# The loops of TensorE's program regrouped: an inner loop over the pair of steps, one choice of projection per group

## The chip, the cores and the metric

One core of a Trainium2 chip runs the whole program. The metric is the device time of one execution in microseconds (us), the median of several runs. PE is TensorE, PEld its weight loads, PEldq the register and branch instructions in the same queue, DVE is VectorE, ACT is ScalarE, POOL is GpSimd, SP is the queue that issues the transfers.

## The reference, cut to what matters

Input x has 2 sequences of 2048 steps with 512 features; `cond` is one vector of 512 per sequence. Four layers follow each other, each with a residual.

```
h0 = cond;  for t: h = tanh(h @ Wh0 + x[t] @ Wx + b)          # a plain recurrence,     x = x + h
w  = softmax over the 2 sequences of (cond . x)/sqrt(512)     # one weight per step,    x = x + x*w
m  = tanh(x @ W_ih.T + cond @ W_hh.T + biases)                # the middle layer,       x = x + m
g0 = cond;  for t: z = sigmoid([x,g] @ Wz + bz);  r = sigmoid([x,g] @ Wr + br)
            c = tanh([x, r*g] @ Wh + bh);  g_new = (1-z)*g + z*c                        # x = x + g_new
            g = tanh(g_new @ Wp + bp) after each 4th step (but the last), else g_new    # "propagation"
```

## The kernel before

The 2048 steps are cut into 128 chunks of 16 steps (`CHUNKS`, `STEPS`). The gated recurrence runs two chunks (`LAG`) behind the plain one, so that in chunk i the program does one step of each, side by side, 16 times. What lies between the two recurrences (softmax over the sequences, middle layer, projection of the gates' inputs) is done for a whole chunk at once, at steps of chunk i that are fixed by hand. Every engine has its own queue in program order, and semaphores that count steps tie the queues together.

**TensorE.** `step` issues four products for one step: `ps_r` (gate r), `ps_z` (gate z), `ps_c` (candidate) and `ps_l` (the plain recurrence, weights and state in three bf16 parts). `ps_r` waits for the state that VectorE's scan leaves (`h_odd` for the first step of a pair, `h_even` for the second). `propagation` is one more product after each 4th step. `softmax_logits` (`ps_proj` from `qx_sum`), `project_mid` (`ps_mid` from `ih`), `project_gates` (`ps_mid` from `rcz_x`, 384 columns) and `project_rnn_input` (`ps_proj` from `rnn_x`) are the chunk's other products.

From chunk 2 on, this is a loop nest with registers: L559 over chunks i, L560 over the four groups q of a chunk, L561 over the two pairs of steps v of a group. The body of the innermost loop is one pair of steps, written out, and behind it a tree of branches (L565 to L581):

```
for v in 0, 1:                       # L561
    two steps
    if v < 1:                        # L565
        if q < 1: softmax_logits     # L566;  else (L568) nothing
    else:
        propagation
        q 0: project_mid;  q 1: project_gates, first half;  q 2: second half;  q 3: project_rnn_input
```

The first two chunks are written out (only the plain recurrence), and the last two (only the gated one) have a nest of the same form at L587. At the head of an iteration the registers for the waits are worked out from i, q and v in one record (FUSED_REGOPS at L561).

**The other engines.** VectorE and ScalarE run a loop over chunks with the 16 steps written out. In a step VectorE transposes each product out of PSUM and ScalarE applies tanh; VectorE's scan (L776) makes the new state. The chunk's extra work stands behind `z_T` of one step: logits and the pair's maximum at u = 2, the reciprocal at u = 3, `mid_T` at u = 5, gate rows at u = 12 and 13. ScalarE does Exp at the end of u = 2 and `mid_tanh` at the start of u = 6. GpSimd adds the results to `y` one step at a time and does the adds and multiplies of softmax and middle layer between them. SP spills and fetches the rows that seed the products.

Of the kernel before, what the change touches and what calls it, by code (L numbers as in the profile page):

```python
# [35 lines left out]
P = 128  # L36
QUAD = 32
NJ = P // QUAD
KT = D // P
STEPS = QUAD // B  # L40
# [12 lines left out]
def cond_resid_kernel(nc, xT, condT, w_rnn_x, w_rnn_h, b_rnn, w_ih, w_hh, b_ih, b_hh,  # L53
# [5 lines left out]
    with ctx:  # L59
# [260 lines left out]
        def _(pool):  # L320
# [29 lines left out]
            def iteration(i):  # L350
# [21 lines left out]
                outputs(i, gru, range(0, 2))  # L372
# [9 lines left out]
                outputs(i, gru, range(2, 3))  # L382
# [8 lines left out]
                outputs(i, gru, range(3, 5))  # L391
# [7 lines left out]
                outputs(i, gru, range(5, 6))  # L399
# [3 lines left out]
                outputs(i, gru, range(6, STEPS))  # L403
# [9 lines left out]
        def _(pe):  # L413
# [95 lines left out]
            def project_gates(i, tiles):  # L509
                if tiles[0] == 0:  # L510
                    pe.wait_ge(x3_new_done, i)
                last = product(ps_mid, ROWS, lambda k: x3_new[:, k, :], lambda k, j: rcz_x[:, k, j, :], 3 * P, tiles)
                if tiles[-1] == KT - 1:
                    last.then_inc(gates_in_product, 1)
# [21 lines left out]
            def projections(i, q):  # L536
                if q == 0:
                    project_mid(i)
                if q in (1, 2):
                    project_gates(i, ((0, 1), (2, 3))[q - 1])  # L540

            for i in range(LAG):
                if i == 1:
                    pe.wait_ge(loaded_gru, 16 * 8)
                for u in range(STEPS):
                    step(True, False, STEPS * i + u, None, u)
                    if i > 0 and u == 1:
                        softmax_logits(i)
                    if u % PROP == PROP - 1:
                        if i > 0:  # L550
                            projections(i, u // PROP)
                        if u // PROP == 3:
                            project_rnn_input(i + 2)
# [5 lines left out]
            with nc.Fori(LAG, CHUNKS, engines=[pe.engine], head_slot={pe.engine: 0}) as i:  # L559
                with nc.Fori(0, GROUPS, engines=[pe.engine]) as q:  # L560
                    with nc.Fori(0, PROP // 2, engines=[pe.engine]) as v:  # L561
                        t = STEPS * i + PROP * q + 2 * v
                        for u in range(2):
                            step(True, True, t + u, t + u - STEPS * LAG, u)
                        with pe.If(v < 1):  # L565
                            with pe.If(q < 1):  # L566
                                softmax_logits(i)
                            with pe.Else():  # L568
                                pe.nop()
                        with pe.Else():  # L570
                            propagation(STEPS * i + PROP * q + PROP - 1 - STEPS * LAG)
                            with pe.If(q < 2):
                                with pe.If(q < 1):
                                    projections(i, 0)
                                with pe.Else():
                                    projections(i, 1)
                            with pe.Else():
                                with pe.If(q < 3):
                                    projections(i, 2)
                                with pe.Else():  # L580
                                    with pe.If(i < CHUNKS - 2):  # L581
                                        project_rnn_input(i + 2)
                                    with pe.Else():
                                        pe.nop()


            with nc.Fori(CHUNKS, CHUNKS + LAG, engines=[pe.engine], head_slot={pe.engine: 0}) as i:  # L587
                with nc.Fori(0, GROUPS, engines=[pe.engine]) as q:
                    with nc.Fori(0, PROP // 2, engines=[pe.engine]) as v:
                        t = STEPS * i + PROP * q + 2 * v  # L590
                        for u in range(2):
                            step(False, True, None, t + u - STEPS * LAG, u)
                        with pe.If(v < 1):
                            with pe.If(STEPS * i + q < STEPS * CHUNKS + 1):
# [340 lines left out]
```

## Time and profile before

| | |
|---|---|
| median of 3 runs | 8982.6 us (8972.62 to 8989.48) |
| the profiled execution | 8973.57 us, its span 8971.7 us |
| PE busy | 8283.6 us, 92% of the span |
| PEld busy | 7582.6 us, 85% |
| DVE busy | 5908.8 us, 66% |
| ACT busy | 4568.0 us, 51% |
| POOL busy | 1071.9 us, 12% |
| mean granted clock of TensorE | 0.995 |

Busy time of PE is that of matmuls that overlap (each takes 0.22 us or more and the next starts long before it ends), so gaps between products are read from start times rather than from busy shares.

### The profile page before, as it was taken

Reading aid. Unit: us, or ns where it says so; the run is one execution under the profiler, and the core shown is the slowest. Engines: PE = TensorE matmul, PEld = TensorE weight load, DVE = VectorE, ACT = ScalarE, POOL = GpSimd, SP = SyncE. Lnnn points to the kernel's source line nnn. Section 1 sums busy time; section 2 is a strip of 40 time slices with the busy share of each in tenths; the row PEclk is TensorE's granted clock in tenths of the full one; section 3 lists DMA queues with packets and bytes.
Section 4 is the critical chain, followed back from the end, with each engine's and each line's share of the span. In section 5 each row is a group of like instructions: output and inputs, shape, how many; then the busy total and the mean of one; then the engine's idle time right before and its main releaser. Section 6 shows DMA issues by size and latency. Waiting matters only on the chain.

```text
span 8971.7 us, 1050872 instructions
## 1 busy us (share of the span) xinstructions
PE 8283.6 (92%) x472080; PEld 7582.6 (85%) x472080; DVE 5908.8 (66%) x34722; ACT 4568.0 (51%) x26367; POOL 1071.9 (12%) x4362
## 2 busy tenths in 40 slices
PE   6999999999999999999999999999999999999998
PEld 5888888888888888888888888888888888888887
DVE  4666666666666666666666666666666666666665
ACT  3555555555555555555555555555555555555554
POOL 1111111111111111111111111111111111111110
PEclk8999999999999999999999999999999999999999
DMA  1000000000000000000000000000000000000000
GB/s 64 10 11 11 10 10 11 12 10 10 11 12 10 10 11 12 10 10 11 12 10 10 11 12 10 10 10 12 10 10 10 13 10 10 10 13 10 10 10 8
DMA packets 133303, 104.84 MB, mean 12 GB/s; under 512 B 14976, under 2 KB 132096, under 8 KB 132096
## 3 DMA queue, kind: packets, MB, share of 16 engines
q1 hardware_dynamic: 133248, 104.20, 3.8%
q8 instruction: 23, 0.38, 0.0%
q14 instruction: 32, 0.26, 0.0%
HBM read 62.20 MB, written 41.94 MB: 12 GB/s over the span
## 4 chain that ended last, share of the span: by engine, by line
PE 92%; issue 7%; DVE 1%; ACT 0%; DMA 0%; SPq 0%; DVEq 0%; ACTq 0%; POOL 0%
PE ps_c L453 27%; PE ps_r L453 23%; PE ps_z L430 20%; PE ps_l L441 16%; PE ps_mid L419 6%; PE ps_proj L419 2%; DVE ps_c L628 0%; PE ps_proj L502 0%; DVE l_T L624 0%; DMA rnn_h<-w_rnn_h 0%; ACT scan_add L866 0%; ACT rnn_hist L828 0%; DVE l_pre L677 0%; DVE l_parts L695 0%; DVE rnn_h L662 0%
## 5 line engine op out<-in xcount | busy, mean ns | idle before, releaser
L453 PE MATMUL ps_c<-c_h,rh 128*2 128x64 f32 x131072 | 2209.7, 219 | 0.3 <-issue 0.3
L453 PEld LDWEIGHTS ps_c<-c_h,rh 128*2 128x2 f32 x131072 | 2037.8, 85 | 14.3 <-issue 0.5
L849 ACT ACTIVATE r_tanh<-ps_r 128x4 f32<-128x4 f32 x4096 | 711.7, 174 | 2500.0 <-DVE ps_r L628 2423.2
L628 DVE STREAM_TRANSPOSE ps_r<-ps_r 128x64 f32<-128x64 f32 x4096 | 1087.2, 265 | 1341.9 <-PE ps_r L453 1217.4
L441 PE MATMUL ps_l<-rnn_h_parts,l_parts 128*6 128x128 bf16 x98304 | 1763.8, 220 | 48.8 <-DVE l_parts L695 42.6
L628 DVE STREAM_TRANSPOSE ps_c<-ps_c 128x64 f32<-128x64 f32 x5118 | 1352.4, 264 | 680.3 <-PE ps_c L453 651.5
L453 PEld LDWEIGHTS ps_r<-r_h,h_odd 128*2 128x2 f32 x65536 | 918.0, 85 | 830.6 <-issue 469.6
L453 PE MATMUL ps_r<-r_h,h_odd 128*2 128x64 f32 x65536 | 1103.5, 219 | 547.4 <-issue 539.2
L441 PEld LDWEIGHTS ps_l<-rnn_h_parts,l_parts 128*6 128x6 bf16 x98304 | 1488.3, 86 | 57.3 <-ACT ps_l L788 48.5
L453 PE MATMUL ps_r<-r_h,h_even 128*2 128x64 f32 x65536 | 1109.3, 219 | 14.7 <-DVE h_even L776 8.8
L430 PE MATMUL ps_z<-z_h,h_odd 128*2 128x128 f32 x32768 | 1088.5, 273 | 0.0
L430 PE MATMUL ps_z<-z_h,h_even 128*2 128x128 f32 x32768 | 1082.3, 273 | 0.0
L453 PEld LDWEIGHTS ps_r<-r_h,h_even 128*2 128x2 f32 x65536 | 906.6, 84 | 94.6 <-DVE h_even L776 39.1
L866 ACT ACTIVATE scan_add<-ps_c 128x4 f32<-128x4 f32 x4096 | 717.8, 175 | 447.0 <-DVE ps_c L628 277.6
L729 DVE SCALAR_TENSOR_TENSOR rh<-r_tanh,h_neg_half 128x4 f32<-128x4 f32 x4096 | 678.9, 166 | 352.1 <-ACT r_tanh L849 351.9
L430 PEld LDWEIGHTS ps_z<-z_h,h_odd 128*2 128x2 f32 x32768 | 825.4, 85 | 15.7
L430 PEld LDWEIGHTS ps_z<-z_h,h_even 128*2 128x2 f32 x32768 | 810.2, 85 | 25.3
L860 ACT ACTIVATE z_tanh<-z_T 128x8 f32<-128x8 f32 x2048 | 429.4, 210 | 599.3 <-DVE z_T L624 599.3
L624 DVE STREAM_TRANSPOSE z_T<-ps_z 128x128 f32<-128x128 f32 x2048 | 647.6, 316 | 59.5 <-PE ps_z L430 10.4
L624 DVE STREAM_TRANSPOSE l_T<-ps_l 128x128 f32<-128x128 f32 x2048 | 632.4, 309 | 46.7 <-PE ps_l L441 46.7
L343 POOL TENSOR_TENSOR y<-x,h_even 128x8 f32<-128x8 f32 x1024 | 212.7, 208 | 3712.9 <-DVE h_even L776 3696.1
L453 PE MATMUL ps_c<-prop_w,h_pre 128*2 128x64 f32 x32704 | 593.9, 219 | 3.7 <-DVE h_pre L776 3.7
(87 smaller groups left out, 9165.5 us busy)
## 6 DMA issues: line engine op xcount, KB each, us to landing
gates_spill<-gates_rows SPq DMA_DIRECT2D x128, 192.0 KB, 1.9
gates_seeds<-gates_spill SPq DMA_DIRECT2D x512, 48.0 KB
x_next<-xT SPq DMA_DIRECT2D x128, 64.0 KB, 1.7
x_mid<-xT SPq DMA_DIRECT2D x128, 64.0 KB, 1.7
rnn_spill<-rnn_rows SPq DMA_DIRECT2D x128, 64.0 KB, 1.5
rnn_seeds<-rnn_spill SPq DMA_DIRECT2D x512, 16.0 KB
y_out<-y SPq DMA_DIRECT2D x128, 64.0 KB, 1.6
rcz_x<-w_rc_x SPq DMA_DIRECT2D x1, 2048.0 KB, 9.2
```

The source lines that it names most:

```text
L343: tt(y[:, :, rows], x3[:, :, rows], h[:, :, :, 1], ALU.add).then_inc(y_ready, 1)
L419: last = nc.tensor.matmul(psum[QUAD * j:QUAD * j + rows, 0:width], stationary(k), weights(k, j), start=(k == 0), stop=(k == KT - 1))
L430: last = nc.tensor.matmul(psum[QUAD * j:QUAD * j + B, 0:P], stationary(k), w[:, k, P * j:P * (j + 1)], start=False, stop=(k == KT - 1), sk ...
L441: last = nc.tensor.matmul(psum[QUAD * j:QUAD * j + PARTS * B, 0:P], state_parts[:, k, :, :].rearrange("p q b -> p (q b)"), w_parts[:, k, j ...
L453: last = nc.tensor.matmul(pair[QUAD * j:QUAD * j + B, n, at:at + W], stationary(k), w[:, k, P * j + W * n:P * j + W * (n + 1)], start=Fals ...
L624: return nc.vector.transpose(tile, psum[:, 0:P])
L628: nc.vector.transpose(pieces[n].rearrange("p k r -> p (k r)"), pair[:, n, at:at + W]).then_inc(T_done[n], inc)
L729: nc.vector.scalar_tensor_tensor(rh[:, k, :], r_tanh[:, k, :], 1.0, h_neg_half[:, k, :], ALU.subtract, ALU.mult).then_inc(rh_ready[n], 1)
L849: nc.scalar.activation(r_tanh[:, k, :], r_T[n][:, :, 0:B], ACT.Tanh, scale=-0.5).then_inc(r_tanh_done[n], 1)
L860: nc.scalar.activation(z_tanh[:, :, :], z_T[:, :, 0:B], ACT.Tanh, scale=0.5).then_inc(z_tanh_done, 1)
L866: nc.scalar.activation(scan_add[:, k, :, 0], c_T[n][:, :, 0:B], ACT.Tanh).then_inc(c_tanh_done[n], 1)
```

## The change

The loop over q now holds three parts one behind the other: a loop over the two pairs of steps with nothing but the pair in it (its counter is the step number itself, with an offset), then the propagation, then one tree of branches that picks the chunk's other product: `softmax_logits` for q 0, `project_mid` for q 1, all of `project_gates` for q 2, `project_rnn_input` for q 3. Softmax so moves from behind step 1 to behind step 3, the middle layer from behind step 3 to behind step 7, and the gates' projection, halved until now behind steps 7 and 11, stands whole behind step 11. The last two chunks and the written-out chunk 1 follow the same order. VectorE, ScalarE and GpSimd take up their parts later: logits at u = 4, Exp at u = 4, reciprocal at u = 5, `mid_T` at u = 8, `mid_tanh` at u = 9; GpSimd's steps are moved in the same way between its sums. No product, transfer or vector operation is added or removed.

```
@@ GpSimd: the same work between the outputs
-                outputs(i, gru, range(0, 2))
+                outputs(i, gru, range(0, 4))
...
-                outputs(i, gru, range(2, 3))
+                outputs(i, gru, range(4, 5))
...
-                outputs(i, gru, range(3, 5))
+                outputs(i, gru, range(5, 8))
...
-                outputs(i, gru, range(5, 6))
+                outputs(i, gru, range(8, 9))
...
-                outputs(i, gru, range(6, STEPS))
+                outputs(i, gru, range(9, STEPS))
@@ TensorE: the projection of the gates in one piece
-            def project_gates(i, tiles):
-                if tiles[0] == 0:
-                    pe.wait_ge(x3_new_done, i)
-                last = product(ps_mid, ROWS, lambda k: x3_new[:, k, :], lambda k, j: rcz_x[:, k, j, :], 3 * P, tiles)
-                if tiles[-1] == KT - 1:
-                    last.then_inc(gates_in_product, 1)
+            def project_gates(i):
+                pe.wait_ge(x3_new_done, i)
+                product(ps_mid, ROWS, lambda k: x3_new[:, k, :], lambda k, j: rcz_x[:, k, j, :], 3 * P).then_inc(gates_in_product, 1)
@@ TensorE: the main nest
             with nc.Fori(LAG, CHUNKS, engines=[pe.engine], head_slot={pe.engine: 0}) as i:
                 with nc.Fori(0, GROUPS, engines=[pe.engine]) as q:
-                    with nc.Fori(0, PROP // 2, engines=[pe.engine]) as v:
-                        t = STEPS * i + PROP * q + 2 * v
+                    behind = STEPS * i + (PROP * q + 2 - STEPS * LAG)
+                    with nc.Fori(behind, behind + PROP, 2, engines=[pe.engine]) as t:
                         for u in range(2):
-                            step(True, True, t + u, t + u - STEPS * LAG, u)
-                        with pe.If(v < 1):
-                            with pe.If(q < 1):
-                                softmax_logits(i)
-                            with pe.Else():
-                                pe.nop()
-                        with pe.Else():
-                            propagation(STEPS * i + PROP * q + PROP - 1 - STEPS * LAG)
-                            with pe.If(q < 2):
-                                with pe.If(q < 1):
-                                    projections(i, 0)
-                                with pe.Else():
-                                    projections(i, 1)
-                            with pe.Else():
-                                with pe.If(q < 3):
-                                    projections(i, 2)
-                                with pe.Else():
-                                    with pe.If(i < CHUNKS - 2):
-                                        project_rnn_input(i + 2)
+                            step(True, True, t + (u - 2 + STEPS * LAG), t + (u - 2), u)
+                    propagation(behind + (PROP - 3))
+                    with pe.If(q < 2):
+                        with pe.If(q < 1):
+                            softmax_logits(i)
+                        with pe.Else():
+                            project_mid(i)
+                    with pe.Else():
+                        with pe.If(q < 3):
+                            project_gates(i)
+                        with pe.Else():
+                            with pe.If(i < CHUNKS - 2):
+                                project_rnn_input(i + 2)
...
@@ VectorE, in the written-out steps
-                    if mid and u == 5:
+                    if mid and u == 8:
                         dve.wait_ge(mid_product, i)
                         transposed(flat(mid_T[:, :, :]), ps_mid).then_inc(mid_T_done, 1)
...
-                    if mid and u == 2:
+                    if mid and u == 4:
                         dve.wait_ge(logit_product, i)
...
-                    if mid and u == 3:
+                    if mid and u == 5:
                         dve.wait_ge(denom_done, i)
@@ ScalarE
-                    if mid and u == 6:
+                    if mid and u == 9:
                         act.wait_ge(mid_pre_done, i)
...
-                    if mid and u == 2:
+                    if mid and u == 4:
                         act.wait_ge(shifted_done, i)
```

## Rows read from the trace of the kernel before

**Rows 1.** Windows: one chunk; busy per engine, granted clock.

```profile
core 0: us, PE busy (x) PEld busy (x) DVE busy (x) ACT busy (x) POOL busy (x), PEclk, DMA share, GB/s
4000.00:4069.00 69.00, 64.42 (x3699) 59.06 (x3693) 46.01 (x272) 35.70 (x208) 8.32 (x34) 1.00 0.03 10
```

**Rows 2.** Waits of PE, 200 to 8820 us (total, times, longest), then from 8820.

```profile
PE ps_r L453 <- issue: 519.4, 748, 1.8
...
PE ps_r L453 <- issue: 10.9, 7, 2.1
```

**Rows 3.** Timeline of PE: l to the next product, within and between pairs.

```profile
4014.61 0.85 PE L441 MATMUL ps_l<-rnn_h_parts,l_parts 128*6 128x128 bf16 x48
4015.31 1.09 PE L453 MATMUL ps_r<-r_h,h_even 128*2 128x64 f32 x64
...
4017.98 0.85 PE L441 MATMUL ps_l<-rnn_h_parts,l_parts 128*6 128x128 bf16 x48
4019.61 1.07 PE L453 MATMUL ps_r<-r_h,h_odd 128*2 128x64 f32 x64 [0.77 <-issue]
...
4069.98 0.85 PE L441 MATMUL ps_l<-rnn_h_parts,l_parts 128*6 128x128 bf16 x48
4070.65 0.27 PE L502 MATMUL ps_proj<-qx_sum,ones 128*32 128x32 f32 x8
4071.48 1.07 PE L453 MATMUL ps_r<-r_h,h_odd 128*2 128x64 f32 x64 [0.56 <-issue]
```

**Rows 4.** Source lines in PE's queue, 4018.3 to 4019.7 us; durations in ns.

```profile
L565 PEldq COMPARE_BRANCH  x1: 67/67/67, 4018.4 to 4018.4; - x1
L566 PEldq COMPARE_BRANCH  x1: 207/207/207, 4018.5 to 4018.5; - x1
L568 PEldq COMPARE_BRANCH  x1: 169/169/169, 4018.8 to 4018.8; - x1
L561 PEldq ALU_OP  x1: 36/36/36, 4019.0 to 4019.0; - x1
L561 PEldq COMPARE_BRANCH  x1: 209/209/209, 4019.1 to 4019.1; - x1
L561 PEldq FUSED_REGOPS  x1: 160/160/160, 4019.4 to 4019.4; - x1
```

**Rows 5.** The same for L560, 4011 to 4012 us.

```profile
L560 PEldq MOVE  x1: 35/35/35, 4011.6 to 4011.6; - x1
```

**Rows 6.** Timeline of PE: ends of the groups q 0, q 1 and q 3.

```profile
4008.56 0.85 PE L441 MATMUL ps_l<-rnn_h_parts,l_parts 128*6 128x128 bf16 x48
4009.35 1.23 PE L453 MATMUL ps_c<-prop_w,h_pre 128*2 128x64 f32 x64
4010.43 1.08 PE L419 MATMUL ps_mid<-ih,x 128*32 128x128 f32 x32
4011.95 1.07 PE L453 MATMUL ps_r<-r_h,h_odd 128*2 128x64 f32 x64 [0.43 <-issue]
...
4025.64 0.85 PE L441 MATMUL ps_l<-rnn_h_parts,l_parts 128*6 128x128 bf16 x48
4026.43 1.15 PE L453 MATMUL ps_c<-prop_w,h_pre 128*2 128x64 f32 x64
4027.56 1.50 PE L419 MATMUL ps_mid<-rcz_x,x_new 128*32 128x384 f32 x16
4028.89 1.07 PE L453 MATMUL ps_r<-r_h,h_odd 128*2 128x64 f32 x64
...
4059.55 0.85 PE L441 MATMUL ps_l<-rnn_h_parts,l_parts 128*6 128x128 bf16 x48
...
4063.78 1.07 PE L453 MATMUL ps_r<-r_h,h_odd 128*2 128x64 f32 x64 [0.80 <-issue]
```

**Rows 7.** Timeline of DVE and ACT, 4018.3 to 4019.7 and 4026.3 to 4029.0 us.

```profile
4018.50 0.48 DVE L776 TENSOR_TENSOR_SCAN h_odd<-scan_mul,scan_add 128x8 f32<-128x8 f32 x2
...
4019.00 0.30 ACT L845 ACTIVATE mid_tanh<-mid_pre 128x128 f32<-128x128 f32 x1
...
4028.07 0.17 ACT L879 ACTIVATE h_odd<-ps_c 128x4 f32<-128x4 f32 x1 [0.25 <-DVE ps_c L628]
```

**Rows 8.** Source line L566 over the whole span; min/median/max in ns.

```profile
L566 PEldq COMPARE_BRANCH  x630: 65/202/3604, 127.9 to 8818.7; - x158
```

More of the change, by code:

```diff
@@ L546, in _ @@
                     step(True, False, STEPS * i + u, None, u)
-                    if i > 0 and u == 1:
+                    if i > 0 and u == 3:
                         softmax_logits(i)
[L549 to L552, printed above, removed]
-                            project_rnn_input(i + 2)
+                    if i > 0 and u == 7:
+                        project_mid(i)
+                    if i > 0 and u == 11:
+                        project_gates(i)
+                    if u == 15:
+                        project_rnn_input(i + 2)
             pe.wait_ge(r_seeded, 1)
@@ L587, in _ @@
             with nc.Fori(CHUNKS, CHUNKS + LAG, engines=[pe.engine], head_slot={pe.engine: 0}) as i:
                 with nc.Fori(0, GROUPS, engines=[pe.engine]) as q:
-                    with nc.Fori(0, PROP // 2, engines=[pe.engine]) as v:
-                        t = STEPS * i + PROP * q + 2 * v
+                    behind = STEPS * i + (PROP * q + 2 - STEPS * LAG)
+                    with nc.Fori(behind, behind + PROP, 2, engines=[pe.engine]) as t:
                         for u in range(2):
-                            step(False, True, None, t + u - STEPS * LAG, u)
-                        with pe.If(v < 1):
-                            with pe.If(STEPS * i + q < STEPS * CHUNKS + 1):
-                                softmax_logits(CHUNKS)
-                            with pe.Else():
-                                pe.nop()
-                        with pe.Else():
-                            with pe.If(STEPS * i + PROP * q < STEPS * (CHUNKS + LAG) - PROP):
-                                propagation(STEPS * i + PROP * q + PROP - 1 - STEPS * LAG)
-                            with pe.Else():
-                                pe.nop()
-                            with pe.If(STEPS * i + q < STEPS * CHUNKS + 2):
-                                with pe.If(STEPS * i + q < STEPS * CHUNKS + 1):
-                                    projections(CHUNKS, 0)
-                                with pe.Else():
-                                    projections(CHUNKS, 1)
-                            with pe.Else():
-                                with pe.If(STEPS * i + q < STEPS * CHUNKS + 3):
-                                    projections(CHUNKS, 2)
-                                with pe.Else():
-                                    pe.nop()
@@ new lines, in _ @@
+                            step(False, True, None, t + (u - 2), u)
+                    with pe.If(STEPS * i + PROP * q < STEPS * (CHUNKS + LAG) - PROP):
+                        propagation(behind + (PROP - 3))
+                    with pe.Else():
+                        pe.nop()
+                    with pe.If(STEPS * i + q < STEPS * CHUNKS + 2):
+                        with pe.If(STEPS * i + q < STEPS * CHUNKS + 1):
+                            softmax_logits(CHUNKS)
+                        with pe.Else():
+                            project_mid(CHUNKS)
@@ L614, in _ @@
+                    with pe.Else():
+                        with pe.If(STEPS * i + q < STEPS * CHUNKS + 3):
+                            project_gates(CHUNKS)
+                        with pe.Else():
+                            pe.nop()
         @block.vector
```

9 lines of the change are left out of this document (3 added, 6 removed).

## The prediction

> **What bounds the kernel now.** I looked first at the busy time of one chunk, then at PE's waits, then at the order of its products in time, last at the register and branch records of its queue. In a chunk of 69.00 us PE is busy 64.42 us at the full granted clock, DVE 46.01 and ACT 35.70 [rows 1]: PE sets the pace. Between 200 and 8820 us it waits almost only for "issue" in front of `ps_r`: 519.4 us in 748 places [rows 2]. The reader is to see where: inside a pair the next `ps_r` starts 0.70 us after `ps_l` (4014.61 to 4015.31); between the pairs of a group it takes 1.63 us (4017.98 to 4019.61), and 1.50 us where softmax's product stands between them (4069.98 to 4071.48) [rows 3]. No data is late there: the scan that makes `h_odd` is done at 4018.98 [rows 7], 0.6 us before `ps_r` starts. The queue is busy with control: six records from 4018.4 to the load at 4019.60 [rows 4]. Their durations sum to 0.85 us, the distance is 1.2 us, so each brings about 0.06 us more to the next. Prices per record, from [rows 4, 5]: compare that falls through 0.067 + 0.06 = 0.13; compare that jumps (L566, and L561's back edge) 0.27; plain jump (L568) 0.23; ALU_OP 0.10; MOVE 0.09; FUSED_REGOPS 0.22. The first of them comes 0.42 us after `ps_l` starts (4017.98 to 4018.4): the queue runs some 0.2 us ahead of the array, and control longer than that shows.
>
> **The inner edge, four per chunk.** Before, one takes 1.50 and three take 1.63 us from `ps_l` to `ps_r` [rows 3]; sum 6.39. The change removes the compare L565 (0.13), the compare L566 (0.27), the jump L568 (0.23) and the index arithmetic of the head (0.22), since the counter is the step number and `ps_r`'s wait needs it unchanged. What is left is one addition (0.10) and the back edge (0.27); the head must still copy the counter (a MOVE, 0.09). So 0.42 + 0.10 + 0.27 + 0.09 = 0.88. The loop's limit is now a register, for which there is no row: nothing if it is kept, one ALU_OP (0.10) if it is worked out at each edge. I take 0.90. Four edges: 3.60. Gain 6.39 - 3.60 = 2.79 us per chunk. Floor: the 0.70 of a pair's inside, where data sets the start; ceiling 0.98.
>
> The Trainium skill (Advanced Engine Details and Errata, Control Flow Timing) gives about 51 ns for a branch and 108 ns for a compare-and-branch. By it the three removed branches would be 0.27 us instead of 0.63, four edges would give 1.4 us less, and the time would be about 8820. The rows show 169 ns and 207 ns for those that jump, and 67 ns for one that doesn't; the measurement decides.
>
> **The ends of the groups.** Before, from `ps_l` to the next `ps_r`: 3.39 (q 0), 3.25 (q 1; q 2 has the same pattern and is taken as 3.25), 4.23 (q 3) [rows 6]; sum 14.12. Afterwards:
> - The way to the propagation stays 0.79 (4008.56 to 4009.35): a jumping compare and an addition become an addition, a compare that falls through and an addition, 0.04 less, which the wait for `h_pre` takes up. From the propagation to the next product it is 1.13 with a jumping compare (4026.43 to 4027.56), so 0.99 with two that fall through.
> - Behind the chosen product there stood: jump, addition, compare falling through, addition, back edge, two MOVEs, index arithmetic = 0.23 + 0.10 + 0.13 + 0.10 + 0.27 + 0.18 + 0.22 = 1.23. Now: jump, addition, back edge, index arithmetic, one MOVE = 0.91. That is 0.32 less. I assume that copying q, start value and limit fit into the one fused record; if each operation is a record of its own, some seven at 0.10 cost 0.5 more.
> - q 0 (softmax): 0.79 + 0.99 + what follows softmax today, 4070.65 to 4071.48 = 0.83 [rows 3], plus the MOVE = 2.70. `h_odd` comes from the propagation here, and softmax is short cover. In q 1 its second half is written from 4028.07 to 4028.24 [rows 7], 1.81 us behind the propagation's start at 4026.43; `ps_r` would start after 0.99 + 0.92 = 1.91, so the state is there by 0.1 us.
> - q 1 (middle layer): 0.79 + 1.13 + (4010.43 to 4011.95 = 1.52, less 0.32) = 3.12.
> - q 2 (all gates): 16 matmuls of 384 columns occupy 1.33 us (4027.56 to 4028.89), and cover their control; 32 take at most 2.66, of which the start-up is paid once: 2.60. 0.79 + 1.13 + 2.60 = 4.52.
> - q 3: 4.23 - 0.32 = 3.91.
>
> Sum 14.25, that is 0.13 more than before: the ends come out even, since one control sequence covered by gates' matmuls is traded for softmax's uncovered one. Net 2.79 - 0.13 = 2.66 us per chunk.
>
> **The moved steps.** VectorE's logits stay behind the first step of a pair (u 2 to 4), and their cost there is the same. The reciprocal goes from u = 3 to 5, ahead of an edge, which is no worse. `mid_T` goes from u = 5 (ahead of an edge with slack) to u = 8 (ahead of a step within a pair); I charge 0.03 us per chunk, at the most the 0.3 that a transpose lasts. `mid_tanh` on ScalarE ran at 4019.00 for 0.30 us [rows 7], 0.5 us after the scan began. At u = 9 the next `ps_r` starts sooner, but ScalarE is wanted only when that product has been transposed, some 1.1 us later, so it stays hidden. GpSimd's part is nearly idle (8.32 of 69 us, [rows 1]) and is asked for one group later, by queues that have a group's time. SP issues the same transfers.
>
> **The sum.** 126 chunks x (2.66 - 0.03) = 331 us. The last two chunks have no `ps_l`, so `ps_r` waits for data longer; all their issue waits are 10.9 us [rows 2], of which I take half, 5. The first chunks: nothing. 331 + 5 = 336. Against the profiled execution's own time: 8973.6 - 336 = 8637.6. The median of the runs stands 9 us above that execution: 8646 by it. I forecast 8640.
>
> **The rivals.**
> - More is won: the edge meets the 0.70 to 0.75 of the inside of a pair, if copy and limit cost nothing or PE's queue gets further ahead. For: nothing else stood in the way inside a pair. Against: the records have to run. 4 x 0.17 x 126 = 86 us more, 8555. Chance 0.10.
> - Less is won, by register work: limit at each edge and the heads' arithmetic unfused: (0.08 x 4 + 3 x 0.48) x 126 = 222 us less, 8860. For: a register limit and a computed start are new. Against: seven operations fit in one record now. Chance 0.10.
> - Less is won, because VectorE and ScalarE needed the pauses. They have 46 us of work in a chunk that would last 66.4, but each step's chain is serial. Against: second steps of a pair run with no pause before them, on time. If half of each edge's gain were eaten: 2.79 / 2 x 126 = 176 us less, 8815. Chance 0.06.
> - Slower: the back jumps miss the code. The longest compare at L566 took 3.604 us, its median 0.202 [rows 8]: a first arrival at cold code. If each group's back jump (four per chunk) paid 3.4 us, the chunk would be 13.6 - 2.6 = 11 us longer, about 10,000 in all. It decides from 0.66 us per group on. Against: today's innermost back edge spans more code than the new one, at 209 ns. Chance 0.04.
> - The change does not do this, since something else holds the edge at today's length: 8970 to 8985. Chance 0.02.
>
> The Trainium skill (Runtime: NRT & Kernel Launch, Instruction fetch mechanics) says that a jump to code outside the current two pages stalls on a fetch, which is the fourth rival's mechanism. The trace shows such a stall only in L566's maximum.
>
> **How the numbers follow.** The forecast as worked out has 0.68; its own range is 8590 to 8700 (edge 0.85 to 0.98, heads 0.1 either way, `mid_T` up to 0.3). To leave out no more than 2 in 10, I take 8555 to 8745: with it go the first rival and the milder cases of the second. A difference of 0.2% (18 us) is about what a measurement of this kernel can tell from none. Faster 0.93, the same 0.03, slower 0.04.
>
> **What would show it.** Right: between the pairs `ps_l` to `ps_r` of about 0.90 us in place of 1.63, behind softmax about 0.9 us, `ps_proj<-qx_sum` now behind the propagation; two records and a MOVE at each edge, and a chunk of 66.4 us. Wrong: waits for DVE in front of `ps_r`, compare records of microseconds in every chunk, or edges that stay above 1.1 us.

## The result, and the profile after

| | before | after |
|---|---|---|
| median of the runs | 8986.04 us (4 runs, 8972.62 to 8992.95) | 8619.63 us (4 runs, 8616.62 to 8622.46) |
| profiled execution | 8973.57, span 8971.7 | 8622.46, span 8620.6 |
| mean granted clock | 0.995 | 0.995 |

The ratio is 0.9594, with an interval of 0.9577 to 0.9611: faster by 4.1%, 20 us below the 8640 forecast and inside the range.

First the page of after: span and instructions, busy times, and the queue that fetches code.

```profile
span 8620.6 us, 1049320 instructions
PE 8290.4 (96%) x472080; PEld 7617.0 (88%) x472080; DVE 5914.3 (69%) x34722; ACT 4570.1 (53%) x26367; POOL 1073.8 (12%) x4362
q8 instruction: 23, 0.38, 0.0%
```

PE's busy time is what it was (8283.6 and 8290.4 us); only its share rose, from 92% to 96%. The same window of one chunk, which answers to [rows 1] with 66.4 us in place of 69:

```profile
4000.00:4066.40 66.40, 64.50 (x3704) 59.33 (x3693) 46.00 (x272) 35.66 (x207) 8.34 (x34) 1.00 0.04 11
```

What PE waited for between 200 and 8480 us (total, times, longest), against [rows 2]:

```profile
PE ps_r L453 <- ACT h_odd L861: 81.0, 125, 0.6
PE ps_r L453 <- issue: 66.7, 157, 1.5
```

The 519.4 us of "issue" (PE waits for its own queue) in 748 places in front of `ps_r` are 66.7 in 157. What is new there, ScalarE's `h_odd`, is one place per chunk, the end of group q 0; whether that name is right is asked below.

PE's products in time. First an edge between two pairs and the inside of a pair ([rows 3]), then the ends of the groups q 1, q 2, q 3 and q 0 (against [rows 6]); start and duration in us:

```profile
4013.26 0.85 PE L441 MATMUL ps_l<-rnn_h_parts,l_parts 128*6 128x128 bf16 x48
4014.15 1.07 PE L453 MATMUL ps_r<-r_h,h_odd 128*2 128x64 f32 x64
...
4016.80 0.85 PE L441 MATMUL ps_l<-rnn_h_parts,l_parts 128*6 128x128 bf16 x48
4017.51 1.09 PE L453 MATMUL ps_r<-r_h,h_even 128*2 128x64 f32 x64
...
4004.00 0.85 PE L441 MATMUL ps_l<-rnn_h_parts,l_parts 128*6 128x128 bf16 x48
4004.78 1.18 PE L453 MATMUL ps_c<-prop_w,h_pre 128*2 128x64 f32 x64
4005.97 1.08 PE L419 MATMUL ps_mid<-ih,x 128*32 128x128 f32 x32
4007.20 1.07 PE L453 MATMUL ps_r<-r_h,h_odd 128*2 128x64 f32 x64 [0.15 <-issue]
...
4020.18 0.85 PE L441 MATMUL ps_l<-rnn_h_parts,l_parts 128*6 128x128 bf16 x48
4020.97 1.12 PE L453 MATMUL ps_c<-prop_w,h_pre 128*2 128x64 f32 x64
4022.09 2.79 PE L419 MATMUL ps_mid<-rcz_x,x_new 128*32 128x384 f32 x32
4024.68 1.09 PE L453 MATMUL ps_r<-r_h,h_odd 128*2 128x64 f32 x64
...
4037.70 0.85 PE L441 MATMUL ps_l<-rnn_h_parts,l_parts 128*6 128x128 bf16 x48
4038.45 1.15 PE L453 MATMUL ps_c<-prop_w,h_pre 128*2 128x64 f32 x64
4040.06 1.08 PE L419 MATMUL ps_proj<-rnn_x,x_next 128*32 128x128 f32 x32 [0.45 <-issue]
4041.63 1.07 PE L453 MATMUL ps_r<-r_h,h_odd 128*2 128x64 f32 x64 [0.48 <-issue]
...
4054.75 0.85 PE L441 MATMUL ps_l<-rnn_h_parts,l_parts 128*6 128x128 bf16 x48
4055.50 1.16 PE L453 MATMUL ps_c<-prop_w,h_pre 128*2 128x64 f32 x64
4056.52 0.27 PE L502 MATMUL ps_proj<-qx_sum,ones 128*32 128x32 f32 x8
4057.44 1.07 PE L453 MATMUL ps_r<-r_h,h_odd 128*2 128x64 f32 x64 [0.65 <-ACT h_odd L861]
```

The reader is to see that the edge is 0.89 us (4013.26 to 4014.15) where it was 1.63, with no wait marked on it any more, and that the inside of a pair is the same 0.71. The ends are 3.20 (q 1), 4.50 (q 2), 3.93 (q 3) and 2.69 (q 0).

The control records of that edge, by source line (durations in ns), against [rows 4]; the inner loop is L555:

```profile
L555 PEldq FUSED_REGOPS  x1: 37/37/37, 4013.7 to 4013.7; - x1
L555 PEldq COMPARE_BRANCH  x1: 213/213/213, 4013.8 to 4013.8; - x1
L555 PEldq MOVE  x1: 37/37/37, 4014.1 to 4014.1; - x1
```

Three records where there were six: a fused record that must hold the addition to the counter and the limit (no other record is left for them; the profile does not show what a fused record holds), the back edge, the copy. And at the head of the group behind q 3's projection:

```profile
L552 PEldq MOVE  x1: 35/35/35, 4041.2 to 4041.2; - x1
L552 PEldq FUSED_REGOPS  x1: 152/152/152, 4041.3 to 4041.3; - x1
```

Where the state stands beside them: the first half of VectorE's scan for the edge at 4014.15 and for the inside of the pair at 4017.51, and the second half of ScalarE's `h_odd` for the end of q 0 at 4057.44:

```profile
4013.74 0.17 DVE L758 TENSOR_TENSOR_SCAN h_odd<-scan_mul,scan_add 128x8 f32<-128x8 f32 x1
...
4017.28 0.17 DVE L758 TENSOR_TENSOR_SCAN h_even<-scan_mul,scan_add 128x8 f32<-128x8 f32 x1
...
4057.16 0.17 ACT L861 ACTIVATE h_odd<-ps_c 128x4 f32<-128x4 f32 x1 [0.25 <-DVE ps_c L610]
```

Inside a pair `ps_r` starts 0.06 us behind the end of that scan (0.054 to 0.055 at each of 960 such places in 120 chunks): there data sets the start. At the edge it starts 0.24 us behind it here (median 0.229 of 480): the data is there, and the control is what is late.

**Where the 351 us came from.** The two spans differ by 8971.7 - 8620.6 = 351.1 us. By the starts of the first `ps_r` of the chunks: the first chunk in which both recurrences run starts at 116.92 before and at 120.04 after (-3.1); from there to chunk 126 it is 8574.63 and 8233.69, for 124 chunks 69.15 and 66.40 us each (340.9); the next two chunks, without a projection of the plain recurrence's input, take 138.26 and 133.51 (4.75); the last two, in which only the gated recurrence runs, 137.8 and 129.2 up to the start of the last product (8.5). 340.9 + 4.75 + 8.5 - 3.1 = 351.1.

Within a chunk, medians of the distances from product to product over 123 chunks, and for the chunk their sum:

| us per chunk | before | after | gain | forecast |
|---|---|---|---|---|
| four edges, `ps_l` to `ps_r` | 1.500, 1.623, 1.624, 1.622 = 6.37 | 0.884, 0.884, 0.882, 0.882 = 3.53 | 2.84 | 2.79 |
| ends of q 0, q 1, q 2, q 3 | 3.388, 3.250, 3.240, 4.318 = 14.20 | 2.690, 3.104, 4.502, 3.927 = 14.22 | -0.03 | -0.13 |
| inside the pairs | | | -0.05 | -0.03 |
| chunk | 69.05 | 66.29 | 2.76 | 2.63 |

### The profile page after: what moved, and what is told of

It reads as the page before. It is cut to its first block, busy times and chain, and to the rows that moved or that the text cites. A ratio compares the mean times of both kernels' runs of the same rounds, so it can differ in the third digit from the quotient of the medians.

```text
span 8620.6 us, 1049320 instructions
## 1 busy us (share of the span) xinstructions
PE 8290.4 (96%) x472080; PEld 7617.0 (88%) x472080; DVE 5914.3 (69%) x34722; ACT 4570.1 (53%) x26367; POOL 1073.8 (12%) x4362
## 4 chain that ended last, share of the span: by engine, by line
PE 95%; issue 3%; DVE 1%; ACT 0%; DMA 0%; ACTq 0%; DVEq 0%; SPq 0%; POOL 0%
PE ps_c L453 27%; PE ps_r L453 24%; PE ps_z L430 21%; PE ps_l L441 16%; PE ps_mid L419 6%; PE ps_proj L419 2%; DVE ps_c L610 1%; ACT h_odd L861 0%; DVE l_T L606 0%; DMA rnn_h<-w_rnn_h 0%; ACT scan_add L848 0%; ACT rnn_hist L810 0%; DVE l_pre L659 0%; DVE l_parts L677 0%; ACTq L860 0%
## 5 line engine op out<-in xcount | busy, mean ns | idle before, releaser
L453 PEld LDWEIGHTS ps_r<-r_h,h_odd 128*2 128x2 f32 x65536 | 935.5, 85 | 407.7 <-issue 199.4
L773 ACT ACTIVATE ps_c<-gates_seeds 128x128 f32<-128x128 f32 x2048 | 563.7, 275 | 0.1
```

The lines of the kernel that those rows point to most:

```text
L453: last = nc.tensor.matmul(pair[QUAD * j:QUAD * j + B, n, at:at + W], stationary(k), w[:, k, P * j + W * n:P * j + W * (n + 1)], start=Fals ...
L773: return nc.scalar.activation(pair[:, :, at:at + W], rows.rearrange("p (h n) -> p h n", h=2), ACT.Copy)
```

## The experiments

The theory: PE's queue issues control and matmuls in one order and runs some 0.2 us ahead of the array behind short products; what is gained is the records taken out at the inner edges, and the moves of the projections gain nothing. The rivals: the new placement of the projections is what pays; the state (VectorE's and ScalarE's chain) is what sets the edge now; code fetches count. The kernel before, run beside them, had a median of 8981 to 8985 us. Ratios are to it. Below, "edge" is `ps_l` to the next `ps_r` between pairs, and u is the step within a chunk, 0 to 15.

### The moves without the loops

Before's loops and tree of branches, with after's placement of every step:

```
                    with nc.Fori(0, PROP // 2, engines=[pe.engine]) as v:
                        t = STEPS * i + PROP * q + 2 * v
                        ...
                        with pe.If(v < 1):
                            with pe.If(q < 1):
-                                softmax_logits(i)
+                                pe.nop()
...
                        with pe.Else():
                            propagation(...)
+                           q 0: softmax_logits;  q 1: project_mid;  q 2: project_gates;  q 3: project_rnn_input
```

> The nest of before (innermost loop over the two pairs, tree of branches in its body) with the schedule of after: softmax, middle layer, whole gates and input projection behind the propagations of q 0 to q 3, and the other engines' steps as late as in after. Theory (the gain lies in the control records at the inner edge): edges stay at 1.63 us (1.50 in q 0), 6.39 in all; the ends of the groups are those of after plus 0.32 each where control isn't covered, about 2.7 + 0.3, 3.2 + 0.3, 4.5, 3.93 + 0.3 = 15.2 against 14.1 before. So 1.1 us per chunk and some 140 us slower than before: 9120. Rival (the later places or the joined gates' projection are what gains): faster than before, below 8950.

Measured: 9120.48 us (9119.05 to 9127.52), ratio 1.0156 [1.0139, 1.0173]. An edge of its timeline:

```profile
4013.79 0.85 PE L441 MATMUL ps_l<-rnn_h_parts,l_parts 128*6 128x128 bf16 x48
4015.41 1.07 PE L453 MATMUL ps_r<-r_h,h_odd 128*2 128x64 f32 x64 [0.77 <-issue]
```

The edges stay at 1.48 (q 0) and 1.62, the chunk is 70.15 us. So the moves by themselves lose 1.1 us per chunk, nearly all of it at the ends of the groups (15.29 us in place of 14.20): three ends now have control that no long product covers, where before two had, and only q 2's end has the gates' product in front of its control. All of the gain, and the repair of this loss, is the shorter control.

### One record more at each edge

```
                        for u in range(2):
                            step(True, True, ...)
+                        with pe.If(i < 3):
+                            pe.nop()
+                        with pe.Else():
+                            pe.nop()
```

> After, with one more compare in the inner loop behind the pair that jumps in every chunk but one, and does nothing. Theory (a record in the queue costs its price fully once the queue's lead is used up): 0.27 us at each of 4 edges and about 0.25 in front of each of 4 propagations, 2.1 us per chunk, 262 us: about 8880. Rival (the edge is set by data or the queue has lead left): less than 0.1 us at each edge, below 8720.

Measured: 8859.42 us (8841.92 to 8863.33), ratio 0.9857 [0.984, 0.9873].

```profile
4006.28 0.85 PE L441 MATMUL ps_l<-rnn_h_parts,l_parts 128*6 128x128 bf16 x48
4007.43 1.08 PE L453 MATMUL ps_r<-r_h,h_odd 128*2 128x64 f32 x64 [0.29 <-issue]
```

The edge goes from 0.884 to 1.146: one jumping compare costs 0.26, as the price list of the prediction has it (0.27). The scan for the next pair now ends 0.49 us before `ps_r` starts, where it was 0.23: the state waits for the control. The four in front of the propagations cost 0.24 to 0.32 there too, of which 0.04 to 0.09 comes back, because the propagation's own second half then finds its data. The chunk is 1.96 us longer. This confirms prices and places; had the state set the edge, the record would have been free.

### The four steps of a group written out

No inner loop at all, so the edge has no control:

```
-                    with nc.Fori(behind, behind + PROP, 2, engines=[pe.engine]) as t:
-                        for u in range(2):
-                            step(True, True, t + (u - 2 + STEPS * LAG), t + (u - 2), u)
+                    for u in range(PROP):
+                        step(True, True, behind + (u - 2 + STEPS * LAG), behind + (u - 2), u % 2)
```

> After, with the four steps of a group written out in the main nest, so that no inner edge is left; the body of the loop over q grows from some 1200 to some 2030 records of PE's queue. Theory: each of the four edges falls from 0.88 us to the 0.71 to 0.75 that a product takes inside a pair, 4 x 0.17 x 126 = 86 us: about 8534. Rival 1 (VectorE and ScalarE need the pauses): some edge stays above 0.8 and a wait for DVE or ACT appears in front of ps_r. Rival 2 (the code must be at hand): issue waits of 1 to 4 us in every group, and a time above 9000.

Measured: 15978.4 us, ratio 1.7788 [1.7758, 1.7818]. The theory's 8534 missed by a factor of nearly two, and the rival of the code fetches won far beyond its bound. Its page (queue, packets, MB, share), then what PE waited for between 200 and 15800 us, then PE's timeline at the end of a group and in the middle of a product:

```profile
q8 instruction: 4553, 74.60, 2.2%
```

```profile
PE ps_r L453 <- issue: 2918.6, 1393, 5.7
PE ps_c L453 <- issue: 1511.9, 1063, 1.9
PE ps_z L430 <- issue: 702.3, 500, 1.6
PE ps_l L441 <- issue: 589.8, 500, 1.5
```

```profile
8009.09 0.27 PE L502 MATMUL ps_proj<-qx_sum,ones 128*32 128x32 f32 x8
8014.48 1.89 PE L453 MATMUL ps_r<-r_h,h_odd 128*2 128x64 f32 x64 [5.12 <-issue]
...
8024.71 0.67 PE L441 MATMUL ps_l<-rnn_h_parts,l_parts 128*6 128x128 bf16 x35 [1.13 <-issue]
```

The queue of code carried 23 packets in after and 4553 here: 4530 more in 504 groups, nine per group, each 74.60 MB / 4553 = 16.4 KB. Five stalls per group, with medians of 1.1 to 1.6 us, stand in the middle of products, and they are 127 or 128 matmuls apart: with their weight loads and the control between them that is 256 records, and each packet carries as many at 64 bytes a record. So a stall stands where a block of 256 records begins. A longer one, 5.1 us here and up to 5.7, stands at the jump back to the group's head. (15978 - 8620) / 504 = 14.6 us per group. A part of it is the clock: its mean is 0.893, against 0.995, and behind the long stall it is granted at 0.50, the lower of its two levels, from 8014.5 to 8019.5 us; there `ps_r` lasts 1.89 us in place of 1.07. How much of the 14.6 us is the clock was not separated. The nest has some 2030 records in PE's queue, after's has 1213 (by a count of the programs; matmuls and weight loads alone are 2000 and 1168), of which nothing is fetched again: between 200 and 8600 us that queue carries 4 packets in after. Where between the two the cliff lies was not tried.

The Trainium skill (Runtime: NRT & Kernel Launch, Instruction fetch mechanics) says that PE holds 2048 instructions, refilled in blocks of 256, and that a jump outside the current two blocks waits for a fetch. The block agrees with the 16.4 KB seen here. By the two blocks after's nest, five of them long, would have to fetch at each back jump; the runs show that it does not. The 2048 alone do not give the cliff either: a nest of some 2030 is below them and is fetched again all the same.

### VectorE's work moved ahead of the edges

Twice, to ask whether VectorE's extra work inside the pairs costs anything, and whether it does ahead of an edge:

```
-                    if u == 0 and mid and next_rnn(i):      # the plain recurrence's rows
+                    if u == 1 and mid and next_rnn(i):
...
-                    if mid and u == 8:                      # mid_T;  mid_tanh 9 -> 10
+                    if mid and u == 9:
...
-                    if mid and u == 4:                      # logits and Exp, first kernel only
+                    if mid and u == 5:
...
-                    if mid and u == 5:                      # reciprocal, first kernel only
+                    if mid and u == 6:
```

> After, with VectorE's extra work moved one step later, so that it stands ahead of an inner edge and not inside a pair: the input rows from u 0 to 1, logits u 4 to 5 (Exp with them), reciprocal 5 to 6, mid_T 8 to 9 (mid_tanh to 10), GpSimd's outputs shifted by one. Theory: inside the pairs it delays ps_r by 0.18, 0.04 and 0.04 us (ps_l to h_even 0.89, 0.75, 0.75 in place of 0.71), and an edge of 0.88 covers that: 0.26 us per chunk, 33 us: about 8587. Rival (the edge has no room either): no difference, 8615 to 8625, with waits for DVE at the edges.

Measured: 8626.99 us (8626.08 to 8630.75), ratio 0.9605 [0.9589, 0.9621]: a miss by 40. The rows' move gives its 0.08 (behind `ps_l` at u = 0: 0.887 to 0.807) and `mid_T`'s its 0.03 (0.044, of which 0.013 comes back in the next product), but the reciprocal now stands inside a pair, and `ps_r` to `ps_z` at u = 7 grew from 0.905 to 1.016; the logits' move gives 0.01 only, since what `ps_r` starts earlier it then waits for the second half of the state. The ends of q 1 and q 3 take 0.015 and 0.045 more, which the edit does not explain.

The second kernel moves only rows and `mid_T`:

> The run before of this kind, with two of its three moves only: the input rows from u 0 to 1 and mid_T from 8 to 9 (mid_tanh to 10); logits, Exp and reciprocal stay as in after, since the reciprocal at u = 6 stood inside a pair and cost 0.11 us there. Theory: 0.08 and 0.03 us per chunk, 14 us: 8606. Rival (what is won inside the pair is lost at the edge): 8615 to 8625.

Measured: 8604.04 us (8603.24 to 8607.52), ratio 0.9578 [0.9562, 0.9594]. That is 16 us less than after; forecast as 14. Rows give 0.08 and `mid_T` 0.04 per chunk. 8 ns at each edge (0.876) came with them; they are not the moves' doing, since the next kernel, which moves nothing on VectorE, has the same 0.876. So a part of the 16 us may not be the moves' either.

### Half of the middle layer's product

```
-                product(ps_mid, ROWS, lambda k: x2[:, k, :], columns(ih)).then_inc(mid_product, 1)
+                product(ps_mid, ROWS, lambda k: x2[:, k, :], columns(ih), P, (0, KT - 1)).then_inc(mid_product, 1)
```

> After, but the middle layer's product leaves out two of its four input tiles (16 of 32 matmuls), so the output isn't the reference's. The product stands in q 1 in front of 0.91 us of control. Theory (it mostly covers control): 0.54 us of matmuls fall away, but the next ps_r can start only 0.91 us behind the jump, so ps_mid to ps_r falls from 1.16 to about 1.0 us: 0.15 to 0.2 us per chunk, 20 to 25 us: 8597. Rival (matmul time is what counts): 0.54 x 126 = 68 us: 8552.

Measured: 8621.1 us, ratio 0.9596 [0.9577, 0.9615], where 8597 was expected. PE's timeline at the ends of q 1 and q 2:

```profile
4005.96 0.64 PE L419 MATMUL ps_mid<-ih,x 128*32 128x128 f32 x16
4006.96 1.07 PE L453 MATMUL ps_r<-r_h,h_odd 128*2 128x64 f32 x64 [0.35 <-issue]
...
4020.69 1.15 PE L453 MATMUL ps_c<-prop_w,h_pre 128*2 128x64 f32 x64
4022.06 2.79 PE L419 MATMUL ps_mid<-rcz_x,x_new 128*32 128x384 f32 x32 [0.21 <-issue]
```

This kernel leaves out two of the middle layer's four input tiles. At q 1 all is as expected: 16 matmuls fewer, some 0.44 us of work, and `ps_mid` to `ps_r` is only 0.18 shorter (1.163 to 0.985): behind it the control sets the time and the product is what is hidden. But at q 2 the propagation to `ps_mid` grew from 1.153 to 1.367, in a place that the edit does not touch. Two later kernels ask why.

### Half of the gates' product

```
-                product(ps_mid, ROWS, ..., lambda k, j: rcz_x[:, k, j, :], 3 * P).then_inc(gates_in_product, 1)
+                product(ps_mid, ROWS, ..., lambda k, j: rcz_x[:, k, j, :], 3 * P, (0, KT - 1)).then_inc(gates_in_product, 1)
```

> After, but the gates' projection leaves out two of its four input tiles (16 of 32 matmuls of 384 columns), so the output isn't the reference's. Theory: half of it still covers its 0.91 us of control, as before the change (1.33 us from ps_mid to ps_r), so all of the matmul time comes back: 2.60 to 1.33, 1.27 x 126 = 160 us: 8460. Rival (control shows again): less than 120 us, above 8500.

Measured: 8453.79 us, ratio 0.941 [0.9391, 0.9429].

```profile
4006.97 1.50 PE L419 MATMUL ps_mid<-rcz_x,x_new 128*32 128x384 f32 x16
4008.27 1.09 PE L453 MATMUL ps_r<-r_h,h_odd 128*2 128x64 f32 x64
```

From 2.596 to 1.306 us: here the full work of 16 matmuls goes (two of the four input tiles are left out of the gates' projection). Behind 384 columns the group's control costs nothing, behind 128 columns of the middle layer it costs what the product does not cover. Both halves of the prediction's reading of the ends so hold.

### The counter used without its copy

The first wait of a pair reads the loop's register itself, and the copy stands behind the first product:

```
+                    with contextmanager(pair_loop)(behind, behind + PROP, 2) as (counter, copied):
+                        halved_product(ps_r, ..., h_odd_ready, counter, r_product, 1)
+                        t = copied()
                        for u in range(2):
-                            step(True, True, ..., u)
+                            step(True, True, ..., u, gate_r=u > 0)
```

> After, with ps_r's first wait in a pair taken straight from the loop's counter register, and the copy of the counter made behind that product, where the queue is ahead. Nothing else changes; one MOVE record is gone from the head. Theory (each record costs its price, here 0.09 us): 0.88 to 0.79 at four edges, and 0.09 at the ends of q 0, q 1 and q 3; q 2 is covered by its matmuls: 7 x 0.09 x 126 = 80 us: 8540. Rival (the edge is at its floor, set by the scan or the start of ps_r): no more than 20 us, above 8600.

Measured: 8565.54 us (8561.8 to 8565.71), ratio 0.9533 [0.9517, 0.9549]. The four edges are 0.790 in place of 0.884: the MOVE, 0.09, was the last thing in front of `ps_r`. So the edges of after are still set by control and not by the state. But the chunk is 0.40 us shorter where 0.63 was taken out of it. The rest is given back, most of it as waits for data: `ps_r` to `ps_z` at u = 6 is 0.930 instead of 0.890 (the second half of the state ends 0.31 to 0.32 us behind the start of `ps_r`, in after 0.22, and the gap stands at the first matmul that needs it), and `ps_l` to `ps_r` at u = 14 is 0.805 instead of 0.709 (`ps_r` starts 0.055 behind the scan); the ends of q 1 and q 3 gain only 0.04 and 0.05. At q 0's end `ps_r` starts 0.085 us earlier than in after, so that the wait which the profile put down to ScalarE's `h_odd` ended with the MOVE: in after its second half is written 0.11 us before `ps_r` starts.

### Counters kept in registers, and that with the vector work moved

Pair counter, limit and the propagation's count live in registers over the whole nest, are raised inside the propagation's product, and the heads have no index arithmetic left; the first wait of a pair reads the counter directly, as in the kernel before this one:

```
+            def bookkeeping():
+                captured[0] = nc.snap(group, ...);  captured[1] = nc.snap(chunk, ...)
+                nc.regs_alu(limit, limit, PROP, op=add)
+                nc.regs_alu(pre, pre, PROP, op=add)
...
+                    halved_product(ps_c, P_AT, ..., prop_w, h_pre_ready, pre, p_product, PROP,
+                                   early=((0, 0), (1, 0)), between=bookkeeping)
```

> After, with the control of the main nest cut down: pair counter, its limit and the propagation's count are registers that run through the whole nest, raised inside the propagation's product where the queue is ahead; so the head of a group works out nothing, and the first waits read the registers directly. Theory: edges 0.88 to 0.79 (0.36 per chunk), behind the chosen product 0.91 to 0.60 us of control (q 1 0.30; q 3 0.39, since the head of a chunk has one record left; q 0 only 0.24, because the propagation's state is then late; q 2 nothing, it is covered), 0.1 in front of the propagations: 1.4 us per chunk, 175 us: 8445. Rival (data sets the starts once control is this short): a wait for ACT or DVE in front of ps_r at every edge, and above 8530.

Measured: 8478.57 us (8476.04 to 8479.21, 5 runs), ratio 0.944 [0.9427, 0.9453].

```profile
4010.53 0.85 PE L441 MATMUL ps_l<-rnn_h_parts,l_parts 128*6 128x128 bf16 x48
4011.32 1.08 PE L453 MATMUL ps_r<-r_h,h_odd 128*2 128x64 f32 x64
```

From the chosen product to `ps_r` it is now 0.613 (q 0), 0.898 (q 1) and 1.212 (q 3), in place of 0.918, 1.163 and 1.566: what was taken out of the heads, the MOVE of 0.09 among it, was worth 0.27 to 0.35 a piece where no long product covers it. The time is 34 us above the expected 8445: the propagations start 0.03 to 0.06 earlier (0.753 to 0.707 behind `ps_l`) and take as much longer or a little more (0.05 to 0.07), and the two late places of the kernel before this one are here too (0.932 at u = 6, 0.808 at u = 14).

With the second kernel's moves of VectorE's work on top:

> The same with VectorE's input rows at u = 1 and mid_T at u = 9. Theory: another 0.11 us per chunk, 14 us: 8431. Rival (an edge of 0.79 us has no room for them any more): the same time as without.

Measured: 8461.43 us (8458.29 to 8463.65, 5 runs), ratio 0.9422 [0.941, 0.9435]. The two gains add up (17 us for the moves, 16 in the kernel without the registers). It leaves out nothing of the reference and is the fastest kernel of the study that leaves out nothing, 5.8% below before and 158 us below after.

### Where the gates' product begins in the code

The nest's first record can be shifted against the blocks of 256 records that the fetching kernel had shown. In the kernel with half of the middle layer's product the gates' matmuls begin 1023 records behind the nest's head, the last record of a block; in after 1055 (both by a count of the program, of which 1008 and 1040 are matmuls and weight loads).

```
-            with nc.Fori(LAG, CHUNKS, engines=[pe.engine], head_slot={pe.engine: 0}) as i:
+            with nc.Fori(LAG, CHUNKS, engines=[pe.engine], head_slot={pe.engine: 96}) as i:     # half of the middle product
...
+            with nc.Fori(LAG, CHUNKS, engines=[pe.engine], head_slot={pe.engine: 224}) as i:    # after itself
```

> The kernel with half of the middle product (which leaves out two of its four input tiles, so the output isn't the reference's) came out at 8621 us, since the gates' first matmul in q 2 started 0.21 us later than in after. Its code had moved: by counting the records of the nest, the gates' block begins 1023 records behind the nest's head (four times 256, less one), and in after 1055. Here the same kernel with the nest's head 96 records further on (head_slot 96 in place of 0). Theory (a product that begins where a fetched stretch of code ends pays about 0.2 us): the 0.21 us is gone, 0.21 x 126 = 27 us: 8595. Rival (it comes from the shorter product itself): 8615 to 8625 as before.

Measured: 8599.44 us (8594.88 to 8604.31), ratio 0.9571 [0.9555, 0.9587]. The first kernel's 0.2 us is gone:

```profile
4006.90 1.16 PE L453 MATMUL ps_c<-prop_w,h_pre 128*2 128x64 f32 x64
4008.06 2.79 PE L419 MATMUL ps_mid<-rcz_x,x_new 128*32 128x384 f32 x32
```

> After, with nothing changed but the nest's head at slot 224, so that the gates' block begins one record short of five times 256. Theory: the gates' first matmul starts 0.2 us later in each chunk, and the time rises by some 27 us: 8647, if the other boundaries stay hidden inside the pair. Rival: 8615 to 8625, the place of the code does not matter.

Measured: 8662.26 us (8657.54 to 8662.71), ratio 0.9638 [0.9622, 0.9654].

```profile
4038.17 1.15 PE L453 MATMUL ps_c<-prop_w,h_pre 128*2 128x64 f32 x64
4039.51 2.79 PE L419 MATMUL ps_mid<-rcz_x,x_new 128*32 128x384 f32 x32 [0.19 <-issue]
```

Put there on purpose, the boundary costs the same 0.20 us per chunk, 25 of the 43 us by which this kernel is slower than after and 15 us more than expected. The code queue carries 23 packets here, as in after: nothing is fetched again. Most of the rest lies behind `ps_l` at u = 2, 8 and 14, 0.04 to 0.05 each, and behind `ps_r` at u = 14, 0.04 (a gap behind its 14th matmul, not at its wait for the second half of the state); that these are boundaries too was not tested. In after the boundaries inside the pairs cost nothing that can be seen. A reading that fits is that a boundary shows where it falls into a stretch of control, since the queue's lead is already used up there; it was not tested by itself, and only this one place, one record short of a multiple of 256, was tried.

## Why the prediction was right

**What bounds the kernel.** Right: PE's queue, by its control records at the edges. One compare more costs what the list says, one MOVE fewer gives what the list says, and the moves without the loops leave the edges where they were. The state was there 0.23 us before `ps_r` started at an edge of after.

**The inner edge.** 0.884 measured, 0.90 forecast from a price list. The step that was open, the price of a limit in a register, came out as nothing: beside the back edge and the copy there is one fused record of 37 ns. Gain 2.84 instead of 2.79.

**The ends.** q 0 2.690 (2.70), q 1 3.104 (3.12), q 2 4.502 (4.52), q 3 3.927 (3.91). The assumption behind them, that the head's seven operations fit in one record, is seen at L552 (one fused record of 152 ns). Within the ends one small step was wrong: the 0.04 less in front of the propagation was to be taken up by the wait for `h_pre`; in q 2 `ps_l` to the propagation fell from 0.785 to 0.753, and it was the propagation itself that took 0.04 more (1.109 to 1.153). The margin of 0.1 us for the state at q 0's end was 0.11. Their sum before was 14.20 and not 14.12: q 3's end took 4.23 in the one chunk that was read, its median is 4.32. So the difference is -0.03 instead of -0.13. At 0.10 x 126 = 13 us this is the largest error of the sum, most of it from reading one sample.

**The moved steps.** 0.05 instead of 0.03 us per chunk, `mid_T` at u = 8 (0.708 to 0.751) being most of it. `mid_tanh` stayed hidden.

**Both ends of the program.** The last two chunks gave 8.5 us instead of 5, the first ones cost 3.1 instead of nothing, which nearly cancels. What in the first chunks takes the 3.1 was not looked for.

**The sum.** The 126 chunks gave 345.7 us where 331 was forecast, 14.7 more, and the two ends of the program 0.4 more; that is the 15.1 us between 8637.6, forecast for the profiled execution, and its 8622.5. The mechanism and the terms were right, and not only the total: none was off by more than 0.10 us per chunk. Edges and ends both came out better than forecast, which is most of the 15. The other 5 us to the 8640 are that this was rounded up from 8637.6 and that the median lies 2.8 us below the profiled execution. Of the last two chunks the 5 us were half of a row, a guess; that they fall short by 3.5 and the first chunks cost 3.1 where nothing was set is a near balance by luck.

**The rivals.** That more is won was false for after: the edge met not the inside of a pair but the MOVE. The kernels without that MOVE and without the heads' arithmetic show how much of it was there to win. Register work: false, one fused record per head. VectorE needing its pauses: false at 0.884, but not empty. At 0.79 the second half of the state begins to be late, by 0.04 to 0.1 at a few places of a chunk, and with what the ends do not give that is a third of the 0.63 us per chunk that was forecast for the MOVE. Back jumps that miss the code: false for after, 23 packets in the whole execution, but a real mechanism one step further: a body of four steps instead of two pays for it in every group. The price set for it, 3.4 us per group, was too low by four times, and its sum was off too: 11 us in each of 126 chunks on 8974 is some 10,360, not 10,000. Such a stall stands in before's trace at two more compares (1.96 us at L559, 1.72 at L594), not only at L566; all three are first arrivals.

## What to carry to other kernels

Where an engine's queue carries control between short products, list the control records with their durations and their distance, and price an edit record by record; read each distance as a median over many repetitions, since one sample was the largest error here. Look at what kind of product stands in front of a control sequence: behind 16 or 32 matmuls of 384 columns it was free here, behind 32 of 128 columns it was not, and leaving out half of that product gave back only 0.18 of its 0.44 us. Before a loop body is written out, count the records of its whole nest.

## What the runs showed of the hardware that was not expected

- A nest of some 2030 records in PE's queue fetches its code again in each iteration (nine packets of 16.4 KB, 14.6 us with the slower clock), one of 1213 fetches none. The stalls stand 127 or 128 matmuls apart, a block of 256 records.
- The stalls of such fetches take the clock along: granted clock 0.893 on average in that kernel, 0.995 in after, and 1.89 instead of 1.07 us for the same 64 matmuls behind a stall of 5.1 us.
- With no code fetched again, a block boundary one record ahead of a product that follows control cost 0.20 to 0.21 us (in two programs, each run with it and without it).
- In before and after a compare that jumps takes some 200 to 220 ns and one that falls through 65 to 85, a plain jump 169. The fused record of an edge, by the code two additions, takes 37 ns, that of a head, some seven operations, 152.
- Inside the pairs `ps_r` starts 0.053 to 0.057 us behind the end of the scan that it waits for, at 960 places each of before, after and three of the kernels here; at the edges it is 0.23 in after and 0.14 without the MOVE. So this distance tells a start that data sets from one that control sets.
